# A fused window-attention and int8 feed-forward kernel: another order of work before the first feed-forward product, weights converted by the transfers, an inverse in PSUM, and 178 products of the identity

## The reference, cut to what matters

```python
# x: (4, 1024, 512) f32.  C = 16, window of 8 x 8 tokens in two branches of 8 channels
def attn(x, qkv_w, conv_w0, conv_b0, conv_w1, conv_b1, proj_w, proj_b, ln_w, ln_b):
    tok = x.reshape(B, H * W // C, C)
    q, k, v = split(tok @ qkv_w)
    # branch 0: channels 0-7, windows 1 x 8; branch 1: channels 8-15, windows 8 x 1
    out = softmax(q * 8 ** -0.5 @ k.T) @ v + (depthwise_conv3x3(v_window) + conv_b)
    att = concat(branch0, branch1) @ proj_w + proj_b
    normed = (att - mean(att)) * rsqrt(var(att) + 1e-5) * ln_w + ln_b
    return transpose(tok + normed, (0, 2, 1)).reshape(B, H, W)

def ffn(x, w_gate, w_up, w_down, s_gate, s_up, s_down):      # int8 weights, 512 x 2048 and 2048 x 512
    fuse = silu((x @ w_gate) * s_gate) * ((x @ w_up) * s_up)
    return (fuse @ w_down) * s_down

x = x + layernorm(attn(layernorm(x), ...))
x = x + layernorm(ffn(layernorm(x), ...))
```

## Time and profile before

| what | value |
|---|---|
| median of 3 runs | 977.5 us |
| profiled execution | 979.6 us |
| its span | 977.9 us |
| mean granted TensorE clock | 0.973 |
| busy: PE / DVE / ACT / POOL | 93% / 85% / 66% / 78% |
| first `gate` product | 113.27 us after the span's start |

### The profile page before, as it was taken

One profiled execution on the slowest core, in us unless ns is written; L12 is line 12 of the kernel. 1 busy time (PEld: TensorE's weight loads), 2 busy tenths in 40 slices (PEclk: granted clock), 3 DMA queues, 4 the chain that ended last, 5 costly groups with the idle time before them and its releaser, 6 DMA issues.

```text
span 977.9 us, 17816 instructions
## 1 busy us (share of the span) xinstructions
PE 913.5 (93%) x6527; PEld 709.7 (73%) x6527; DVE 835.1 (85%) x1072; ACT 642.2 (66%) x1143; POOL 759.1 (78%) x725
## 2 busy tenths in 40 slices
PE   3655799999999999999999999999999999989996
PEld 3534688778787878778787878778787877867774
DVE  4899899989999999999999999999989986994322
ACT  2788686758686776758676686758676664845432
POOL 2688689797979889797979879697979885866432
PEclk9976799999999999999999999999999999999998
DMA  4422130120303131130313222130303030111200
GB/s 120 154 83 58 29 88 23 46 84 2 104 28 87 45 78 52 43 88 1 103 29 86 66 47 63 38 93 2 99 11 87 1 87 1 45 44 26 62 20 25
DMA packets 68887, 54.94 MB, mean 56 GB/s; under 512 B 40384, under 2 KB 56768, under 8 KB 68800
## 3 DMA queue, kind: packets, MB, share of 16 engines
q1 hardware_dynamic: 63936, 53.49, 20.3%
q10 hardware_dynamic: 4864, 0.32, 0.3%
HBM read 37.02 MB, written 16.78 MB: 55 GB/s over the span
## 4 chain that ended last, share of the span: by engine, by line
PE 64%; DVE 19%; POOL 7%; issue 4%; ACT 3%; ACTq 1%; DMA 0%; POOLq 0%; DVEq 0%
PE ps_gate L580 17%; PE ps_acc L599 16%; PE ps_up L580 16%; DVE prod L1003 6%; PE ps_w L541 6%; DVE cent L1058 3%; PE ps_w L561 3%; PE ps_w L532 2%; POOL y L931 2%; DVE mid L1101 2%; PE ps_w L571 2%; DVE ps_x L1010 2%; DVE attn L1010 2%; PE ps_w L550 1%; DVE yst L1112 1%
## 5 line engine op out<-in xcount | busy, mean ns | idle before, releaser
L868 POOL TENSOR_TENSOR sum<-prod 128x1024 f32<-128x1024 f32 x128 | 302.4, 2365 | 57.9 <-DVE prod L1003 54.2
L1003 DVE TENSOR_TENSOR prod<-ps_x,qkvl 128x2048 f32<-128x2048 f32 x128 | 290.9, 2277 | 9.7 <-ACT ps_x L693 9.4
L599 PE MATMUL ps_acc<-wd,mid 128*128 128x512 f16 x1024 | 242.3, 380 | 0.0
L580 PE MATMUL ps_up<-xhi,wu 128*128 128x256 f16 x1024 | 231.2, 273 | 3.0 <-DVE mid L1101 3.0
L580 PE MATMUL ps_up<-xlo,wu 128*128 128x256 f16 x1024 | 231.3, 273 | 0.0
L580 PE MATMUL ps_gate<-xhi,wg 128*128 128x256 f16 x1024 | 230.5, 273 | 0.6 <-ACT mid L763 0.6
L580 PE MATMUL ps_gate<-xlo,wg 128*128 128x256 f16 x1024 | 230.5, 273 | 0.0
L936 POOL TENSOR_TENSOR mid<-mid 128x512 f16<-128x512 f32 x128 | 148.6, 1162 | 69.7 <-ACT mid L769 69.7
L763 ACT ACTIVATE mid<-ps_gate,sgate 128x256 f32<-128x256 f32 x256 | 106.9, 468 | 143.8 <-PE ps_gate L580 143.2
L599 PEld LDWEIGHTS ps_acc<-wd,mid 128*128 128x128 f16 x1024 | 100.5, 99 | 96.4 <-issue 1.3
L1101 DVE SCALAR_TENSOR_TENSOR mid<-ps_up,sup,mid 128x256 f32<-128x256 f32 x256 | 110.9, 475 | 64.3 <-PE ps_up L580 54.4
(11 more groups left out here) (140 smaller groups left out, 1295.8 us busy)
## 6 DMA issues: line engine op xcount, KB each, us to landing
xrow<-in_L_attn_x SPq DMA_DIRECT2D x16, 512.0 KB, 4.3
xb<-in_L_attn_x SPq DMA_DIRECT2D x128, 64.0 KB
attn_rows<-ratt SPq DMA_DIRECT2D x32, 256.0 KB, 2.6
o<-attn_rows SPq DMA_DIRECT2D x32, 256.0 KB, 3.5
xr<-in_L_attn_x SPq DMA_DIRECT2D x16, 512.0 KB, 4.8
out_x<-y SPq DMA_DIRECT2D x15, 512.0 KB, 4.8
mid<-in_L_ffn_w_gate SPq DMA_DIRECT2D x1, 1024.0 KB, 7.0
mid<-in_L_ffn_w_up SPq DMA_DIRECT2D x1, 1024.0 KB, 9.2
```

The source lines that it names most:

```text
L580: mm = nc.tensor.matmul(ps[:, ROWS * i:ROWS * i + ROWS], w[:, k, P * j:P * j + P], xs[:, n % 2, k, :], start=(k == 0 and part == 0), stop= ...
L599: return nc.tensor.matmul(ps_acc[q][:], f[:, m % SPLITS, ROWS * i + P * q:ROWS * i + P * q + P], wd[:, 2 * m + i, :], start=(m == 0 and pa ...
L868: nc.gpsimd.tensor_tensor(sum4[:, u % 2, :].rearrange("p (s c) -> p s c", c=4), s[:, :, 0:4], s[:, :, 4:8], ALU.add).then_inc(half_done, 1)
L1003: nc.vector.tensor_tensor(prod[:, half].rearrange("p (s j k) -> p s j k", j=WIN, k=WIN), left[:, :, None, :].broadcast_to([P, 4 * WIN, WIN ...
```

## The change

1. **The first norm.** All raw rows of tile 0 are loaded to the second buffer (`raw_row`), so that neither ACT nor DVE overwrites what the other still reads: ACT's four pieces of `apply` and DVE's four no longer wait for each other. `load_xb` of tile 1 waits for both.
2. **Converting transfers.** `load_weights` and ACT's `cast` go. `cast` is now a POOL step: twelve transfers that POOL issues, each of which reads int8 and writes f16 straight into `wg`, `wu`, `wd`. Four stand at the very front of POOL's order, eight later. `gate`, `up` and `down` wait for their own weights.
3. **ACT's first instructions.** A small activation right after the first issue brings the table load forward. The loads of the scales move from ACT's queue to SP, and late (`load_scales`). The derivation of the scales moves from the front of `START` to its middle, among the first products of tile 1.
4. **The inverse in PSUM.** In `cent_out` DVE writes the reciprocal to a `ps_w` bank and multiplies `cent` by it from there; so `cent_out` takes part in the rotation of the two banks. The multiplication by `ln_w` becomes a step of its own on POOL (`cent_lnw`) and runs before DVE's, not after it.
5. **Products of the identity.** Eleven `warm` steps with 14, 6, 10, 32, 20, 12, 18, 6, 16, 10 and 24 products, a twelfth with 10: 178 in the prologue, on a part of `ps_acc` that nothing else uses then. The 8 ahead of the first `gate` stay.
6. **New tables** `START`, `PLAN` and `OWN`. `START` now also holds `cat` and `proj` of tile 1, `qk` of tile 2's third unit and its first `qk_sum`.

```diff
-        START = [("taps", 0), ("masks", 0), ("load_row", 0), ("stats", 0), ("blocks", 0), ("load_xb", 0),
+        START = [("taps", 0), ("cast", 0, 0), ("cast", 0, 1), ("cast", 0, 2), ("cast", 0, 3), ("stats", 0),
+                 ("masks", 0), ("load_row", 0), ("warm", 0, 14), ("blocks", 0), ("warm", 0, 6), ("spread", 0),
...
         def raw_row(n, h):
-            if n == 0 and h >= WIN // 2:
+            if n == 0:
                 return xb[:, 1, h, :].rearrange("p (t c) -> p t c", c=C)
...
-            def load_weights(n, *_):
-                for dst, w, loaded in zip(staged, (w_gate, w_up, w_down), s_wload):
+            def load_scales(n, *_):
+                sp.dma_start(sdown[:], s_down.rearrange("(o n) -> o n", o=1).broadcast_to([P, W])).then_inc(s_scale, 16)
+                for dst, src in ((sgate, s_gate), (sup, s_up)):
...
-            def cast(n, i, bank):
-                w, k = i // KB, i % KB
...
-                nc.scalar.activation(dst[:, part], staged[w].bitcast(I8)[:, part], ACT.Copy).then_inc(w_cast, 1)
...
             act.dma_start(wsm, qkv_w).then_inc(s_const, 16)
+            act.wait_ge(pool_zero, 14)
+            nc.scalar.activation(idle[:], negone[:], ACT.Copy)
...
+            def cast(n, i, bank):
+                w, k = i // KB, i % KB
+                if w < 2:
+                    dst, src = (wg, wu)[w][:, k], (w_gate, w_up)[w].bitcast(I8)[P * k:P * k + P]
+                else:
+                    dst = wd[:, KB * k:KB * k + KB]
+                    src = w_down.bitcast(I8)[KB * P * k:KB * P * k + KB * P].rearrange("(m p) n -> p m n", p=P)
+                pool.dma_start(dst, src).then_inc(s_wload[w], 16)
...
-            def cent_out(n, bank):
+            def cent_lnw(n, bank):
                 if n == 0:
                     pool.wait_ge(lnw_done, 1)
-                pool.wait_ge(cn_done, n + 1)
+                pool.wait_ge(sq_done, 2 * n + 2)
...
             def cent_out(n, bank):
                 dve.wait_ge(crs_done, n + 1)
-                nc.vector.reciprocal(crs[:], crs[:]).then_inc(crs_chain, 1)
+                if bank.last:
+                    need(dve, *released(bank.last))
+                inverse = bank.ps[:, 0:WIN * WIN]
+                nc.vector.reciprocal(inverse, crs[:]).then_inc(crs_chain, 1)
                 dve.wait_ge(crs_chain, n + 1)
+                dve.wait_ge(lnw_chain, n + 1)
...
```

More of the change, by code:

```diff
@@ L35 @@
 FIRST_CONSTS = 3
-LATER = 9
-CASTS = 3 * KB
+LATER = 6
 SETUP_POOL = 3
@@ L254, in times @@
             return 16 * (n // 2) + 16
-        WORK = ("spread", "xt", "qkv", "cat", "proj", "norm1_add", "fx")
+        WORK = ("spread", "xt", "qkv", "cat", "proj", "cent_out", "norm1_add", "fx")
         def released(step):
@@ new lines, in sandwich_kernel @@
+        PLAN = [(-150.00, ("load_row",)), (-134.99, ("stats",)), (-115.83, ("spread",)), (-108.62, ("load_xb",)),
+                (-96.69, ("apply",)), (-82.26, ("xt", 0, 0)), (-76.15, ("xt", 0, 1)), (-70.77, ("qkv", 0, 0)),
+                (-66.85, ("qkv", 0, 1)), (-66.30, ("qkv", 0, 2)), (-64.65, ("token_bias",)),
+                (-63.46, ("xt", 1, 0)), (-63.26, ("qkv", 0, 3)), (-61.98, ("qkv", 1, 0)), (-60.83, ("xt", 1, 1)),
+                (-58.20, ("qx", 0)), (-57.42, ("qkv", 1, 1)), (-56.83, ("qkv", 1, 2)), (-56.78, ("qkv", 1, 3)),
+                (-51.52, ("qk", 0)), (-50.11, ("qk", 1)), (-49.09, ("qx", 1)), (-48.56, ("qk_sum", 0)),
+                (-48.42, ("qk", 2)), (-48.39, ("qk", 3)), (-46.67, ("qk_sum", 1)), (-46.25, ("qk_sum", 2)),
+                (-45.14, ("softmax", 0)), (-43.64, ("exp", 0)), (-43.63, ("qk_sum", 3)), (-41.33, ("pv", 0)),
+                (-40.31, ("softmax", 1)), (-39.39, ("pv", 1)), (-39.27, ("exp", 1)), (-36.90, ("pv_sum", 0)),
+                (-36.65, ("pv", 2)), (-36.55, ("recip",)), (-34.82, ("pv_sum", 1)), (-33.93, ("pv_sum", 2)),
+                (-32.90, ("pv", 3)), (-28.78, ("attn_out",)), (-28.48, ("pv_sum", 3)), (-25.09, ("cat", 0)),
+                (-24.64, ("proj", 0)), (-24.51, ("att_store",)), (-23.77, ("cat", 1)), (-23.77, ("square", 0)),
+                (-23.75, ("load_xr",)), (-21.83, ("proj", 1)), (-21.04, ("square", 1)), (-20.74, ("cent_var",)),
+                (-19.05, ("cent_std",)), (-19.03, ("cent_lnw",)), (-16.98, ("cent_out",)),
+                (-10.16, ("ffn_norm1",)), (-8.76, ("norm1_add", 0)), (-6.51, ("norm1_add", 1)),
+                (-5.86, ("ffn_norm2",)), (-3.55, ("norm2_apply",)), (-2.93, ("fx", 0)), (-1.10, ("fx", 1)),
+                (6.29, ("keep_x1",)), (32.17, ("finish",)), (34.63, ("finish_apply",)), (35.33, ("finish_add",))]
@@ L896, in cent_out @@
                                         ALU.mult).then_inc(lnw_chain, 1)
-                pool.wait_ge(lnw_chain, n + 1)
+            def cent_out(n, bank):
+                pool.wait_ge(cn_done, n + 1)
                 pool.wait_ge(xl_done, n + 1)
@@ L960, in _ @@
                                     pattern=[[C, WIN + 2]], channel_multiplier=-1).then_inc(tokens_done, 1)
[L962 to L963 removed]
+            walk({"stats": stats, "spread": spread_stats, "scales": scales, "cast": cast, "token_bias": token_bias, "qk": qk, "pv": pv, "attn_out": attn_out,
+                  "cent_lnw": cent_lnw, "cent_out": cent_out, "ffn_norm1": ffn_norm1, "ffn_norm2": ffn_norm2, "finish": finish,
                   "finish_last": finish_last, "finish_add": finish_add, "fuse_lo": fuse_lo})
```

225 lines of the change are left out of this document (101 added, 124 removed), and 11 rows, old and new, of the table OWN.

## The result

The changed kernel takes 974.76 us in the median of 7 runs (973.53 to 975.74); the kernel before took 979.07 in the same series (977.06 to 979.88). The ratio is 0.9963, 95% interval 0.9953 to 0.9973: 4.3 us between the medians, and 3.6 us by the ratio. The forecast was a gain of 6.9 us, to 970.6. The profiled execution took 974.9 us, its span 973.2, against 979.6 and 977.9 before.

The account below looks back on a forecast made before the run. The prediction saw a 113.3 us prologue bound by the start, then DVE and POOL, plus 864.6 us in which PE works 849.3. Terms -3.8 (earlier gate), -3.1 (cat, proj) and 0 gave -6.9, 970.6 us, range 964 to 979.

Parts of the forecast that it names:

- The start: Before the first attention product: earlier table load and statistics start that product at 23, 7.2 us earlier.
- The first four also share the transfer engines with the second row load: At the start: POOL's first four converting transfers may cost the first product 1 to 3 us, covered only by the range.
- the walk: Prologue: following all engines' new orders with traced durations put the first gate at 109.5 instead of 113.3 us.
- From the first product to `gate`: Prologue: DVE's 76.6 us of work become 83.7, spending 3.4 of the 7.2 us gained at the start; net -3.8.
- the scale derivation, twenty small instructions (2.1): DVE between first product and gate: the moved derivation of the scales adds 2.1 us of work.
- `gate` not before 112: First gate, forecast near 109.5: arriving no earlier than 112 us would show the walk through the orders wrong.
- rival A: POOL's order: its transfer issues are dear, up to 4.12 us each, ending at about 999 us; chance 0.10.
- `cat` and `proj` moved ahead: Tile 1's cat and proj move from behind gate into the prologue, where PE waits anyway: -3.1 us.
- Behind `gate`: After the first gate: PE is full, so DVE work saved by the inverse in PSUM is off the path; 0.
- rival D: Behind gate: DVE with 27 us less to do removes 5 of PE's 7 us of idle, 965.6 us; chance 0.13.
- The last tile: At the last fx: PE would wait 4.9 us, where it idled 4.7 from 860 to 925; put at nothing.
- Rival B: Prologue: 32 identity products ahead of tile 1's first xt hold PE, 4 us in all, 974.6 us; chance 0.14.

Follow-up runs that it names:

- Experiment 2: The changed kernel with the first four converting transfers moved from POOL's very start to behind its first token bias; 971.44 us, ratio 0.9929.
- experiment 1: The changed kernel with the scale loads and the scale derivation moved early, the loads behind the second row load; 970.59 us, ratio 0.9923.
- Experiment 6: The changed kernel with three DVE instructions of the scale derivation written as TENSOR_TENSOR with two SBUF inputs, places unchanged; 974.52 us, ratio 0.9956.
- experiment 5: The changed kernel with scale loads and derivation early and the first four converting transfers behind the first token bias; 970.58 us, ratio 0.9917.
- experiment 9: The changed kernel with early scale derivation and the first four converting transfers late and apart, scales step behind a value product pair; 966.66 us, ratio 0.9873.
- experiment 3: The changed kernel with the inverse deviation back in SBUF, tables, banks and waits as changed; 980.50 us, ratio 1.0021.
- experiment 12: The changed kernel's tables with the norm's old code: inverse in SBUF, POOL multiplying by ln_w behind DVE again; 1003.39 us, ratio 1.0248.
- experiment 10: The changed kernel with the row statistics 4.8 places later in every tile; 974.40 us, ratio 0.9949.
- experiment 11: The kernel before with only the inverse put in PSUM, tables and POOL's code as before; 993.12 us, ratio 1.0134.
- experiment 4: The changed kernel without its 178 products of the identity, all twelve warm steps out; 978.18 us, ratio 0.9993.
- experiment 7: The changed kernel with early scale derivation, late first four converting transfers, and without the first 14 identity products; 970.53 us, ratio 0.9919.

## Why the prediction was right in sign and wrong in size

The sign was partly luck. Up to the first `gate` the changed kernel is 3.3 us behind the kernel before, where the forecast had it 3.8 ahead. The gain of tile 0, which was forecast, takes 2.5 of that back. It comes out faster only by the 5.5 us behind tile 1's first `gate` product, and the forecast had put that term at nothing.

**The start: the size was off.** `ln` was forecast at 12.5 and came at 11.9; the forecast delay of `conv_w` by 2.3 us was only 0.4 (DVE reads it at 5.67 instead of 5.28): ACT loads the table from 1.28 on, beside POOL's fills, and issues `conv_w` at 2.12. But "The first four also share the transfer engines with the second row load; that is in the range (1 to 3 us on the first product)" was the term that decided, and it met the raw rows of tile 0 as well as the row loads. Experiment 2 puts its price at 3.8 to 4.7 us, above the range given; without it the first product starts at 20.8, so the rest of the walk was 2.2 us too late. The third row's statistics begin at 22.16, in experiment 2 at 19.13, and PE's side was later still.

**From the first product to `gate`: the step that failed.** The walk took +3.4 us for this stretch; it was +8.0. The loss lies in its first part. DVE's first norm of the feed-forward half was to end 72.5 us behind the first product (95.5 less 23), and took 77.3:

```profile
102.65 0.25 DVE L1072 BATCH_NORM_AGGREGATE fmv<-fst 128x2 f32<-128x6 f32 x2
```

From there to the `gate` product 13.8 us passed where the walk had 14.0, so POOL's new order cost what was said. In the first part the walk had "the scale derivation, twenty small instructions (2.1)". The first ten of them alone took 5.5 us (64.36 to 69.89), three holding 4.57 where the same three took 0.68 in experiment 1; with the seven behind them (71.02 to 71.78 and 75.11 to 75.44) it is 6.6. Experiment 1 gets back 4.0 us by the place alone, 1.9 more than the term was given. The stretch is then 87.1 us, 3.9 above before, where the walk less its 2.1 would be 84.4. These other 2.7 us are the second thing that it had wrong, "DVE stays fed nearly throughout": with the derivation gone DVE still waits, for POOL's sums above all. The price of the small instructions was taken from their place in the kernel before, where POOL was idle, and carried into a stretch where POOL is busy 83% of the time (72.92 of 88.10). I had used this very rule for `cent` and did not apply it to small instructions. The text had named the sign of this: "`gate` not before 112". The Trainium skill ("SBUF — State Buffer", Who interferes with whom) says that a tensor_scalar, copy or cast in the fast mode takes the port pair that it shares with GpSimd exclusively and that the loser stands for the whole instruction. The trace agrees (the six rows under experiment 1). The Trainium skill names two-input instructions as contending too, in the same section. Experiment 6 agrees in two of three, with 0.88 and 1.29 us.

**POOL's issues** were under the 1.0 us taken; rival A is out. The first four in the changed kernel, and the dearest single one:

```profile
3.98 2.40 POOL L852 DMA_DIRECT2D wg<-in_L_ffn_w_gate  x4
94.06 0.86 POOL L852 DMA_DIRECT2D wd<-in_L_ffn_w_down  x1
```

The rule of the Trainium skill that the prediction weighed ("SBUF — State Buffer", SBUF: two separate sides), by which a VectorE operation that holds the shared port keeps GpSimd from writing descriptors, is not tested by these durations: beside none of the twelve issues ran a VectorE copy or tensor_scalar. Their place matters more than their price: lumped ahead of a sum they cost DVE 2.7 us, apart nothing (experiments 5 and 9).

**`cat` and `proj` moved ahead: right.** They stand at 109.8 to 113.6, ahead of `gate`, and tile 0 behind it is 2.5 us shorter, where 3.1 was forecast. Where the 0.6 us between them went is open.

**Behind `gate`: forecast 0, measured about -5.** Ten tiles gave 4.1 us. This is the size of rival D, to which I had given 0.13, but not its reason, a DVE with less to do: in the kernel before PE's four selection products of a tile waited for POOL's mask. In tile 3, POOL and PE, before and then after:

```profile
306.18 2.51 POOL L931 TENSOR_TENSOR y<-y,xr 128x512 f32<-128x512 f32 x2
308.65 0.24 POOL L827 TENSOR_TENSOR rmask<-hmask,rrs 128x32 f32<-128x32 f32 x1
308.94 0.62 PE L515 MATMUL ps_w<-rmask,rowsel 128*128 128x16 f32 x4 [0.18 <-POOL rmask L827]
```

```profile
284.67 0.24 POOL L821 TENSOR_TENSOR rmask<-hmask,rrs 128x32 f32<-128x32 f32 x1
285.62 0.52 PE L514 MATMUL ps_w<-rmask,rowsel 128*128 128x16 f32 x4
```

The listed idle is 0.2 us, but from the start of the product ahead of the four to the start of the one behind them 0.92 us pass before and 0.48 after. The same is so in nine of the ten tiles. In the tenth, tile 2, the kernel before has 0.48 and takes 54.76 us as well. Nine times 0.45 is the whole 4.1. What made the mask early is the new order of POOL's work. Before, POOL wrote the mask straight behind the two additions of `finish_add` (`y`), and after, 0.95 us before PE wants it. Neither edit of the norm is needed for it in the new tables: in experiments 3 and 12, with the inverse in SBUF and with the old code of the norm, the distance is 0.48 in each of these tiles, as it is in experiment 10 with the statistics' place changed. It is 0.48 in experiment 11 too, in the tables of before, but there PE is held elsewhere and reaches the four later. Which entries of the tables carry it was not found. What the norm's edits do is to keep these tables from losing more than the mask gives (experiments 3 and 12). The other 1.4 us, behind the `gate` product of tile 11, were not followed up.

**The last tile: the sum right, the place in part.** Forecast 4.9 us of waiting at the last `fx` in place of 4.7 before; measured 65.0 - 59.9 = 5.1 from 860 to 925, of which only 2.09 at `fx` (this row), 1.57 at the `gate` behind it and 1.1 at an `up`:

```profile
913.54 1.09 PE L570 MATMUL ps_w<-ident,o 128*128 128x128 f32 x8 [2.09 <-ACT o L737]
```

**The identity products: right that they cost nothing, wrong that their clock gives only 1.5 us.** Rival B is out; without them the kernel is 3.4 us slower, 2.2 of it before `gate` (experiment 4).

In sum: the start was 2.5 us too good, the stretch 4.6 too good, the rest behind `gate` 4.9 too bad; forecast -6.9, span -4.7.

## What to carry to other kernels

When small VectorE instructions are moved, price them by what GpSimd does at the new place. Three that take 0.2 us each took 0.9 to 2.3 here, each as long as the GpSimd operation beside it, and a form with two inputs gave nothing. So put them where GpSimd waits. Transfers with nothing urgent in them should not start beside the first loads that the kernel waits for, and their issues should be spread over an engine's own gaps. Where an order by table and an edit were made for each other, undoing one of them measures the mismatch and not the edit; look in the trace for the wait that came back before calling the difference the edit's share.

## What was not expected of the hardware

- The hold is passed on, not divided: with three instructions reshaped, the fourth, a TENSOR_SCALAR of 128x16, took 2.31 us instead of 0.16 (experiment 6). TENSOR_SCALAR on one column per partition (L1182, 128x1, at 66.15) took 0.15 us beside a running POOL operation, and a COPY from PSUM (L1206, at 75.11) 0.15.
- Four converting transfers, 2 MB written in all, held other loads back by 3.5 us or more at the start (raw rows used at 12.4, as soon as the statistics were there, instead of 15.9; in experiment 1, with the same four in front, at 14.85), though the issuing engine was busy only 2.4 us with them.
- The clock at the end differs between executions whose last tiles are the same code. Changed kernel and experiment 7, from 905 to 925 us (length, PE busy, clock, transfers):

```profile
905.00:925.00 20.00, 16.34 (x113) 0.91 0.01 2
```

```profile
905.00:925.00 20.00, 16.72 (x128) 1.00 0.01 2
```

PE waits nearly alike in both (the two longest waits are 2.1 and 1.6 us in the first, 1.7 and 1.6 in the second), yet the clock fell in the first alone; what decides it is open. It was 0.83 there in experiments 4 and 5. From tile 14's `gate` to the end 111.7 us pass in experiment 7 and 114.6 in experiment 5. Medians of kernels that differ by less than 1 us are not told apart by such runs: experiments 5 and 7 have the same median, and `gate` products 2.5 us apart.
